# Sixteen GELUs of a block, taken two at a time in the fused scan and MLP

## The reference

```python
# L2_attn: deltaA = exp(dt * A), deltaBx = dt * B * xs, 512 channels x 16 states
h = dA * h + dBx;  y = sum over states of h * C
y = (y + D * xs) * silu(z);  out = y @ out_proj.T
# L2_ffn: 1024 hidden channels
h = silu(x @ w1.T * s1) * (x @ w2.T * s2)
h = gelu(h @ h1.T * s_h1, approximate=False)
h = gelu(h @ h2.T * s_h2, approximate=False)
out = h @ w3.T * s3
```

## Time and profile before

| what | value |
|---|---|
| time, median of 3 runs | 4359.9 us (4356.67 to 4363.57) |
| the profiled execution: its own time | 4317.54 us |
| the profiled execution: span from first to last instruction | 4315.7 us |
| mean granted TensorE clock | 0.960 |
| busy share of the span: PE, DVE, ACT, POOL | 92%, 77%, 67%, 46% |
| one step of the fused part, from one z to the next | 184.9 us |

### The profile page before, as it was taken

One profiled execution on the slowest core, in us unless ns is written; L12 is line 12 of the kernel. 1 busy time (PEld: TensorE's weight loads), 2 busy tenths in 40 slices (PEclk: granted clock), 3 DMA queues, 4 the chain that ended last, 5 costly groups with the idle time before them and its releaser, 6 DMA issues. The chain is left out here.

```text
span 4315.7 us, 100840 instructions
## 1 busy us (share of the span) xinstructions
PE 3985.7 (92%) x39408; PEld 2128.4 (49%) x39417; DVE 3321.2 (77%) x5680; ACT 2878.3 (67%) x4588; POOL 1998.7 (46%) x1891
## 2 busy tenths in 40 slices
PE   8899999888959757899999999999999999999897
PEld 4344444565638423354544445455454555555555
DVE  7899999686665569888888888886137888888586
ACT  5577777664553465888888888875125777777664
POOL 6222222251335635888888888886001222222332
PEclk9899999999969878899999999999999999999999
DMA  5211111105235345455555555654223222222100
GB/s 148 64 39 39 40 40 40 27 28 131 66 119 159 99 113 123 124 155 160 149 169 147 149 146 156 171 149 136 87 90 106 67 64 62 61 70 61 31 13 27
DMA packets 263805, 412.40 MB, mean 96 GB/s; under 512 B 52731, under 2 KB 139802, under 8 KB 263170
## 3 DMA queue, kind: packets, MB, share of 16 engines
q1 hardware_dynamic: 228966, 375.81, 31.2%
q0 software_dynamic: 6912, 18.88, 1.7%
q10 hardware_dynamic: 27456, 11.28, 1.2%
HBM read 351.85 MB, written 53.24 MB: 94 GB/s over the span
## 5 line engine op out<-in xcount | busy, mean ns | idle before, releaser
L2984 POOL TENSOR_TENSOR l_dbx<-l_u,l_bc 128x1024 f32<-128x1024 f32 x256 | 603.4, 2358 | 251.9 <-DVE l_u L3494 83.2
L1169 DVE CUSTOM_DVE_ANT_0 banks<-banks,l3s_table 128x1024 f32<-128x1024 f32 x512 | 619.4, 1241 | 88.7 <-PE banks L1089 84.3
L1252 ACT ACTIVATE l3s_probs<-banks 128x512 f32<-128x512 f32 x1024 | 540.3, 595 | 203.7 <-PE banks L1118 100.4
L1164 DVE TENSOR_REDUCE l0s_peak<-banks 128x1 f32<-128x1024 f32 x512 | 605.3, 1214 | 58.4 <-PE banks L1089 58.0
L1252 ACT ACTIVATE l0s_probs<-banks 128x512 f32<-128x512 f32 x1024 | 535.6, 600 | 165.0 <-PE banks L1089 163.3
L3292 ACT ACTIVATE banks<-l_dt,l_decay 128x512 f32<-128x512 f32 x512 | 346.7, 687 | 223.1 <-DVE banks L3505 220.6
L2994 POOL TENSOR_TENSOR l_ys<-l_ys,l_hc 128x1024 f32<-128x1024 f32 x203 | 479.6, 2363 | 22.2 <-DVE l_hc L3516 22.0
L3166 PE MATMUL banks<-l_ha,l_ring 128*128 128x512 f32 x1024 | 446.6, 593 | 3.6 <-issue 3.6
L3166 PE MATMUL banks<-l_hb,l_ring 128*128 128x512 f32 x1024 | 443.1, 593 | 1.4 <-ACT l_hb L3257 0.9
L3505 DVE TENSOR_TENSOR_SCAN banks<-banks,l_carry,l_dbx 128x512 f32<-128x512 f32 x256 | 319.2, 1278 | 68.9 <-ACT banks L3292 62.0
L1089 PE MATMUL banks<-l3s_q_st,l3s_k_st 122*32 122x512 bf16 x4096 | 346.7, 381 | 4.9 <-ACT l3s_probs L1252 1.0
(11 more groups left out here) (535 smaller groups left out, 7201.7 us busy)
## 6 DMA issues: line engine op xcount, KB each, us to landing
l_bc<-l_bc_rows SPq DMA_DIRECT2D x256, 512.0 KB, 5.3
l_ring<-in_l2f_stream SPq DMA_DIRECT2D x176, 512.0 KB, 6.5
l3s_table<-bias_table SPq DMA_DIRECT2D x16, 960.0 KB
qk_parts<-l0s_probs SPq DMA_DIRECT2D x96, 128.0 KB, 2.4
qk_parts<-l3s_probs SPq DMA_DIRECT2D x32, 384.0 KB, 3.5
y_rows<-l1f_out_b SPq DMA_DIRECT2D x80, 128.0 KB, 1.8
l0s_q_st<-qk_parts SPq DMA_DIRECT2D x64, 96.0 KB
l0s_k_st<-qk_parts SPq DMA_DIRECT2D x64, 96.0 KB
```

Of the source, the lines that this page charges most:

```text
L1164: nc.vector.tensor_reduce(out=peak[:, b % 2, t:t + 1], in_=s1[t % 2], axis=AX, op=ALU.max, negate=True).then_inc(s1_used, 1)
L1169: nc.vector.tensor_tensor_reduce(out=s1[t % 2], in0=s1[t % 2], in1=rows, scale=1.0, scalar=LOW, op0=ALU.add, op1=ALU.max, accum_out=peak[: ...
L1252: nc.scalar.activation(columns(probs[b % 2][:, t, :], half * 512, (half + 1) * 512), scores, ACT.Exp, scale=scale).then_inc(s2_used, 1)
L2984: nc.gpsimd.tensor_tensor(dbx[:, at:at + 2], u[:, 2 * mh:2 * mh + 2], bc[:, load % BR, 0].unsqueeze(1).to_broadcast([P, 2, TB]), ALU.mult)\
```

## The change

GELUs 0 to 12 are done at the unit that `FUSED["gelu"]` names in the step itself, GELUs 13 to 15 at the unit that it names in the next step. The change rewrites this one list; nothing else is touched, and PE's order and the banks stay as they are.

```diff
@@ -2653,7 +2653,7 @@
     "xt": 27,
     "x": [30, 33, 37, 39],
     "xs": [35, 38, 40, 46],
-    "gelu": [32, 35, 38, 42, 44, 47, 49, 50, 58, 59, 61, 62, 63, 5, 11, 11],
+    "gelu": [35, 35, 42, 42, 47, 47, 50, 50, 59, 59, 62, 62, 63, 11, 11, 11],
     "xp": 49,
     "gated": [46, 63],
     "post_stats": 5,
```

## The result

| what | before | after |
|---|---|---|
| median | 4360.0 us (4 runs, 4356.67 to 4363.57) | 4535.2 us (4 runs, 4531.87 to 4538.33) |
| ratio | 1 | 1.0405 (95% interval 1.0392 to 1.0418) |
| mean granted clock | 0.960 | 0.942 |
| fused part in the profile, from the first scan to the first matmul behind it | 1565.8 to 3184.7: 1618.9 us | 1605.8 to 3404.7: 1798.9 us |

The kernel is 175 us slower; 177 were forecast. The fused part is 180 us longer in the profiles.

The account below looks back on a forecast made before the run. PE, with about 3.2 us idle a step, was taken to bound the kernel. Waits of 126 us, 50 for the clock and 1 for step 8 gave 177, added to 4359.9: 4537 us, range 4505 to 4570.

Parts of the forecast that it names:

- What bounds the kernel: In a fused step PE is busy 181.74 of 184.90 us, so speeding other engines gains at most about 3.2 us.
- What is removed: 84 GELU table loads of 1.283 us, 108 us of ACT's time, taken as worth zero apart from 0.5 us a step.
- Wait A: In steps 1 to 6, hid2 on PE waits for GELU 0, moved to unit 35: 7.2 us late.
- Wait B: In steps 1 to 6, hid4 on PE waits for GELU 2, moved to unit 42: 8.4 us late.
- ACT waited for PE at line 3270 twice: Sign expected in the profile after: two such waits, about 5 us and more the first time.
- Wait C: In steps 2 to 7, hid15 on PE waits for GELU 13, moved to unit 11: 12.8 - 6.9 = 5.9 us.
- The clock: PE's clock falls to half behind each of 18 idle times, costing 2.8 us more each, 50 us in all.
- The sum: 126 us for the waits less 0.5 us a step, 50 for the clock, 1 for step 8: 177 us slower.
- The 1 us for step 8: In steps 8 and 9 GELU 13 comes at most 1 us later; 1 us was counted for step 8.
- That no other group would wait: Apart from hid2, hid4 and hid15, PE's groups were taken to wait nothing; otherwise 2 to 4 us a step more.
- The base: Timed runs lie 42 us above the profiled execution of 4317.5 us; the same 177 was added to their median, 4359.9.

Follow-up runs that it names:

- spare_pairs: Kernel before with only GELUs 4, 6, 8 and 10 moved, to units 47, 50, 59 and 62: 4350.5 us against 4352.4.
- gelu2_late: Kernel before with GELU 2 alone moved, from unit 38 to 42: 4413.5 us, ratio to before 1.0133.
- gelu13_late: Kernel before with GELU 13 alone moved, from unit 5 to 11: 4419.5 us, ratio to before 1.0150.
- hid14_twice: Changed kernel with the eight matmuls of hid14 done twice in steps 2 to 7: 4521.0 us against the changed kernel's 4533.8.

## Why the prediction was right, and where it was not

**What bounds the kernel.** Right, and shown from two sides: work taken from ACT alone gave 2 us (spare_pairs); idle time put into PE cost at least its full length each time.

**What is removed.** 84 loads were forecast, 84 are gone. Their worth was put at nothing, and spare_pairs measured 2 us with an interval that holds zero.

**Wait A**, 7.2 us forecast, 6.9 to 7.2 measured; alone it gave the expected time. The reading that decided it was that unit 35 hangs on DVE's gapless chain: ACT had less to do and its exponential there still waits for the scan of unit 33 (0.48 us, before and after).

**Wait B**, 8.4 forecast, 8.61 measured. Its tie to the end of in3 held, also with hid2 on time (gelu2_late): there PE comes to in3 without a wait, and ACT, which has no GELU 2 to do at unit 38, comes to `take_x` 3 early and waits 1.87 us for in3. ACT waited for PE at line 3270 twice, as forecast, 8.21 and 2.82 us.

**Wait C**, 5.9 forecast, 7.6 to 7.8 measured. The mechanism was right, and the size was off because the step was tied to the wrong event. The prediction said that ACT's take of y "then waits for PE's y". It doesn't: ACT comes 0.6 us after y is filled (2387.46, behind an exponential that waited for a scan), and from there to the end of the first GELU at unit 11 there are 13.88 us and not the 12.76 of the sum. What comes last in between is the shift of the norm of y from POOL, which stands behind POOL's products of the new step. The last gating product on DVE, before and after:

```profile
2257.88 1.23 DVE L3439 TENSOR_TENSOR l_xs<-l_xs,l_zs 128x1024 f32<-128x1024 f32 x1
```

```profile
2376.26 1.23 DVE L3439 TENSOR_TENSOR l_xs<-l_xs,l_zs 128x1024 f32<-128x1024 f32 x1
```

From its end to the end of the first GELU at unit 11 are 2282.27 + 0.69 - 2259.11 = 23.85 us before and, with the GELUs at 2400.65, the same 23.85 us after. POOL's first product of the new step starts right behind that gating product, and its work on the norm of y starts 15.2 us behind it both times. Said before gelu13_late ran, this tie gave 8.8 us of waiting there; 8.7 to 9.1 were measured.

**The clock**, 2.8 us for each of 18 waits forecast. Measured are 1.9 to 2.6 at hid2, 2.4 to 2.6 at hid15 and 1.7 to 2.0 at hid4: somewhat less. hid14_twice shows it as a cost that goes away with the idle time.

**The sum.** 6 x (7.05 + 8.61 + 7.72 - 0.5) = 137 us of waits and 6 x (2.4 + 1.9 + 2.5) = 41 us by the clock, together 178, against 180 in the profile's fused part. 126 and 50 were forecast. The 1 us for step 8 isn't there: from z of step 7 to the first matmul behind the fused part there are 3404.68 - 3056.07 = 348.61 us after and 3184.66 - 2835.53 = 349.13 before. That no other group would wait held: in the step shown PE's other idle times are 2.2 us together. The term for C was too small by 11 us and the term for the clock too large by 9, and the two nearly cancel in 177: the closeness of the total is partly luck. A and B were each right to about 0.2 us.

**The base.** I took the 42 us between the timed runs and the profiled execution of before for a cost of timing. That was wrong. In every other kernel the profiled execution's own time lies within the range of the timed runs. The profiled execution of before had its first scan at 1565.8 us, in the other eleven profiles of this case it starts between 1599.1 and 1610.6: that one execution was some 40 us shorter ahead of the fused part. Since the same sum was added to the median, it did no harm.

## What to carry to other kernels

Before work is moved to a later place to save an engine's overhead, find out which buffer it empties and when the bounding engine needs that buffer; with PE 98% busy in a step, each microsecond past that point was paid in full, here 6 times per wait, and the table loads saved on ACT, which has idle time, were worth next to nothing. Count the clock's answer to the wait too: behind each wait of 4 us and more that was put into these steps, the next group took 1.5 to 3.0 us longer, the clock at half where it was read. And tie each event to what really comes last before it: a forecast of a wait is as good as the event that it is measured from.

## What was not expected of the hardware

A wait of the same 3.48 us was followed by no slower group in two steps out of six, and by groups 1.8 to 2.7 us slower in the others. Of the six waits of 4.09 us none was free. Why the same wait sometimes brings the clock down and sometimes doesn't, no run here shows.

Ahead of the fused part, the same code took some 40 us less in one profiled execution than in eleven others. In all eleven, whatever the kernel, PE stands idle there for 21.4 to 22.5 us once, in the mixture of experts; in most of them no engine or transfer ends that idle time. Timeline of PE, changed kernel:

```profile
1488.61 1.22 PE L1855 MATMUL banks<-l1f_acc,ident 128*128 128x256 f32 x2 [22.11 <-issue]
```

The profiled execution of before has no such idle time; its longest at this line is 7.69 us. In the changed kernel DVE has two idle times of 18.6 and 17.6 us in the same place, likewise ended by nothing that the profile shows, and these make up most of the 40 us. What they are was not tried and stays open; they lie outside the change, and the comparisons are of medians over several runs.
